# An attention block on one core: the pair sums of probabilities are dropped, and norm work moves from VectorE to ScalarE and GpSimd

## The reference, cut to what matters

```python
mod = silu(c) @ wmod                      # six rows of 512 for each batch: sa, ca, ga, sb, cb, gb
h = layernorm(x) * (1 + ca) + sa          # the "head" of a batch
q, k, v = split(h @ W_qkv + b_qkv)        # q and k are then turned (rope)
att = softmax(causal(q @ k.T / sqrt(32)))
x = x + ga * ((att @ v) @ W_proj + b_proj)
h = layernorm(x) * (1 + cb) + sb          # the "tail" of a batch
y = layernorm(h) * ln_g + ln_b            # (the reference's routed part adds nothing to h here)
out = x + gb * y
```

## Time and profile before

| | us |
|---|---|
| median of three timed runs | 3326.5 (3326.02 to 3330.23) |
| the profiled execution, its own time | 3331.65 |
| its span, first to last instruction | 3329.9 |

### The profile page before, as it was taken

The page is one execution under the profiler, slowest core; times in us unless marked ns, Lnnn a source line. Parts: engine busy times, 40 slices in busy tenths (PEclk is TensorE's granted clock), DMA queues, the critical chain, the costliest instruction groups (busy, mean ns, idle before and its releaser), DMA issues.

```text
span 3329.9 us, 59017 instructions
## 1 busy us (share of the span) xinstructions
PE 3022.2 (91%) x21664; PEld 1154.2 (35%) x21664; DVE 2585.6 (78%) x4454; ACT 1759.3 (53%) x3411; POOL 1575.2 (47%) x1489
## 2 busy tenths in 40 slices
PE   3799999999989999999998999999898999999895
PEld 1323333324343433424333242433324333242221
DVE  4697777897768788897877878798776878878477
ACT  3416565656655555655455555565544555555551
POOL 2304343471616365372644726365471655627354
PEclk8759999999999999999999999999999999999997
DMA  5402030313041220413123041311314112031122
GB/s 207 106 10 66 20 69 19 92 39 75 13 103 39 70 57 23 100 39 84 39 52 93 26 94 33 80 50 39 87 33 109 42 45 72 26 77 45 48 75 69
DMA packets 180874, 205.27 MB, mean 62 GB/s; under 512 B 21460, under 2 KB 137428, under 8 KB 179428
## 3 DMA queue, kind: packets, MB, share of 16 engines
q1 hardware_dynamic: 180584, 201.50, 23.0%
HBM read 114.09 MB, written 36.50 MB: 45 GB/s over the span
## 4 chain that ended last, share of the span: by engine, by line
PE 46%; DVE 20%; issue 16%; POOL 6%; POOLq 5%; DVEq 3%; DMA 2%; ACT 1%; SPq 1%; ACTq 0%
DVE mpart L864 11%; PE ring L1108 9%; PE ps_out L1158 9%; PE ps_scores L1144 7%; PE ps_scores L1082 6%; PE ps_den L1175 4%; PE ps_scores L1094 3%; PE ring L1130 3%; PE ps_den L1181 3%; POOL psum L504 3%; DVE dsum L880 2%; POOL psum L503 2%; DVE wk L908 1%; POOLq L484 1%; DVE wk L906 1%
## 5 line engine op out<-in xcount | busy, mean ns | idle before, releaser
L699 ACT ACTIVATE prob<-ps_scores 128x512 f32<-128x512 f32 (+3 forms) x2560 | 1261.8, 537 | 1128.8 <-PE ps_scores L1147 548.6
L864 DVE TENSOR_REDUCE mpart<-ring 128x1 f32<-128x512 f32 (+3 forms) x2560 | 1399.4, 599 | 277.2 <-PE ring L1108 143.0
L1108 PE MATMUL ring<-qk 96*128 96x512 f16 (+3 forms) x2560 | 877.6, 364 | 91.0 <-DVE mpart L864 79.1
L1144 PE MATMUL ps_scores<-qk 98*128 98x512 f16 (+3 forms) x2560 | 865.5, 352 | 35.5 <-ACT prob L699 31.5
L503 POOL TENSOR_TENSOR psum<-prob 128x512 f32<-128x512 f32 x360 | 482.4, 1340 | 427.3 <-ACT prob L699 296.3
L1158 PE MATMUL ps_out<-prob,v 128*32 128x512 f32 (+3 forms) x5120 | 608.0, 547 | 0.0
L1108 PEld LDWEIGHTS ring<-qk 96*128 96x128 f16 x2560 | 235.7, 97 | 909.8 <-DVE mpart L864 666.7
L504 POOL TENSOR_TENSOR psum<-prob 128x512 f32<-128x512 f32 x360 | 481.8, 1338 | 0.0
L1144 PEld LDWEIGHTS ps_scores<-qk 98*128 98x128 f16 x2560 | 246.5, 98 | 347.0 <-ACT prob L699 213.1
L1082 PE MATMUL ps_scores<-hT,wg 128*128 128x512 f16 x1536 | 345.2, 382 | 3.5 <-POOL hT L494 3.5
L522 POOL TENSOR_TENSOR xs<-xs,bc 128x512 f32<-128x512 f32 x60 | 77.1, 1286 | 553.7 <-DMA xs<-in_L_attn_x_dram 552.8
(11 more groups left out here) (122 smaller groups left out, 2568.2 us busy)
## 6 DMA issues: line engine op xcount, KB each, us to landing
qk<-half SPq DMA_DIRECT2D x384, 128.0 KB, 3.5
turn<-in_rope_dram SPq DMA_DIRECT2D x64, 512.0 KB, 4.6
xs<-in_L_attn_x_dram SPq DMA_DIRECT2D x124, 256.0 KB, 2.8
attn_out_T<-ot SPq DMA_DIRECT2D x63, 256.0 KB, 2.1
otin<-attn_out_T SPq DMA_DIRECT2D x30, 512.0 KB, 4.7
out_dram<-x SPq DMA_DIRECT2D x60, 256.0 KB, 2.1
wg<-w_qkv_halves SPq DMA_DIRECT2D x16, 768.0 KB, 5.6
qk<-in_L_wmod_dram SPq DMA_DIRECT2D x1, 6144.0 KB, 26.7
```

Of the source, the lines that this page charges most:

```text
L699: act.activation(prob[:, s % 3, p, h % 2, 0:w], ps_scores[(HG * s + h) % NBK][:, 0:w], ACT.Exp, scale=SCALE).then_inc(exp_done, 1)
L864: dve.tensor_reduce(mpart[:, h, qt, kc:kc + 1], ring[n % NBK][:, 0:w], AX.X, ALU.max).then_inc(ring_free, 1)
L1108: mm = pe.matmul(ring[n % NBK][:, 0:w], qk[0:R, G % 2, 0, h, qt * P:(qt + 1) * P], qk[0:R, G % 2, 1, h, kc * QC:kc * QC + w], start=True, ...
L1144: mm = pe.matmul(ps_scores[k % NBK][:, 0:w], qk[0:RM, par, 1, h, kt * P:(kt + 1) * P], qk[0:RM, par, 0, h, cq * QC + q0:(cq + 1) * QC], st ...
```

## The change

1. `add_pair`, `psum2` and the semaphores `pair_sum` and `pair_used` go. Every step has its own denominators quad from `prob`.
2. `prob` has four buffers; ScalarE waits for the denominators of the step four before.
3. Order on TensorE: values and denominators of the step before stand together, after scores 3, in every step.
4. Tail norms: VectorE keeps the gate product and both statistics. GpSimd makes at step +2 the inverse deviation and minus mean times it; ScalarE applies both in one instruction at step +3 (`tail_scaled1`), between the exponentials of heads 1 and 2; GpSimd multiplies and adds the rows at +4 (`tail_rows1`); statistics at +6; GpSimd again at +6 (`tail_shifts2`); ScalarE at +7 (`tail_scaled2`); GpSimd the last two instructions at +8 (`tail_rows2`).
5. Head in g = 2: ScalarE does the norm (after the exponential of head 2 in the odd step before the tile's) and `head_evac` (in the odd step after it, behind the exponential of head 0). The ring bank of a head tile is therefore freed by ScalarE; `bank_free` on TensorE waits for `ring_free` or `turn_free` accordingly. GpSimd's low half is one step later.
6. The loads of the tile at step 2 are issued inside the projection stretch, at chunk 2, ahead of the load of the last rope table.
7. The planner's loads follow: the added quad, and VectorE without the moved work. The batch loops are counted in one running number of ring uses.

```diff
-    PAIRS = [s for s, (cq, kt) in enumerate(STEPS) if kt < TPC * cq and kt % 2 == 0]
-    NP = len(PAIRS)
+    NPB = 4
+    FIRST_TAIL = 2
@@ product_load, vector_load
-            if STEPS[s - 1][1] >= TPC * STEPS[s - 1][0]:
-                load += 4.2 * width(s - 1)
-        return load + 4.2 * (s - 3 in PAIRS) + 6 * (s in tail) + 2 * (s in head)
+            load += 4.2 * width(s - 1)
+        return load + 6 * (s in tail) + 2 * (s in head)
-        load += sum(c * (s - at in tail) for at, c in ((0, 1.7), (2, 2.2), (4, 4), (6, 2.2), (8, 4)))
-        return load + 2.7 * (s in head) + 2.2 * (s + 2 in head) + (s + 1 in head)
+        load += sum(c * (s - at in tail) for at, c in ((0, 1.7), (2, 2.2), (6, 2.2)))
+        return load + 2.2 * (s + 2 in head)
@@ SyncE, qkv
+                    if c == 2:
+                        tail_load()
                     if G < NG * B - 1 or c < NC_ - 1:
                         load_turn(NC_ * G + c + 1)
@@ GpSimd
+            def minus_mean(to, mean, inverse):
+                pool.tensor_tensor(to, mean, neg_one[:], ALU.mult)
+                pool.drain()
+                return pool.tensor_tensor(to, to, inverse, ALU.mult)
+            def tail_shifts1(b, t):
+                i = t % 2
+                pool.wait_ge(tail_stats1, NT * b + t + 1)
+                inv_std(rstd[:, i, :], mv[:, i, :])
+                pool.drain()
+                minus_mean(shift[:, i, :], mv[:, i, 0:1], rstd[:, i, :]).then_inc(tail_rstd1, 1)
+                pool.tensor_tensor(xs[:, i, :], x1[:, i, :], bc[:, 5, :], ALU.add)
+            def tail_rows1(b, t):
+                i = t % 2
+                pool.wait_ge(tail_n1, NT * b + t + 1)
+                pool.tensor_tensor(wk[:, i, :], wk[:, i, :], bc[:, 2, :], ALU.mult)
+                pool.drain()
+                pool.tensor_tensor(wk[:, i, :], wk[:, i, :], bc[:, 3, :], ALU.add).then_inc(tail_h2, 1)
...
-                        if s - 1 in PAIRS and nxt:
-                            add_pair(G, PAIRS.index(s - 1))
-                        for stage in (0, 1, 3):
-                            if s - 2 * stage in tail:
+                        for stage in (0, 2, 4, 6, 8):
+                            if s - stage in tail:
@@ ScalarE
-                            act.wait_ge(prob_used, wait_value(S - 2 if s >= 3 else NS * G))
+                            act.wait_ge(prob_used, wait_value(S - NPB + 1))
...
+                            if h == 1 and s - 3 in tail_at(g, b == 0, last):
+                                tail_scaled1(b - 1, tail_at(g, b == 0, last)[s - 3])
+                            if h == 1 and s - 7 in tail_at(g, b == 0, last):
+                                tail_scaled2(b - 1, tail_at(g, b == 0, last)[s - 7])
+                            if h == 0 and s - 1 in head:
+                                head_evac(b + 1, head[s - 1], turns[s - 1])
+                            if h == 2 and s + 1 in head:
+                                head_normed(b + 1, head[s + 1])
+            def head_evac(b, t, use):
...
+                act.wait_ge(head_done, NT * b + t - 1)
+                act.wait_ge(ring_full, use + 1)
+                for k in range(KC):
+                    scaled = act.activation(x1[:, t % 2, k * P:(k + 1) * P], ring[use % NBK][:, k * P:(k + 1) * P],
+                                            ACT.Identity, bias=colmod[:, 0, k:k + 1], scale=colmod[:, 1, k:k + 1])
+                scaled.then_inc(turn_free, 1)
+            def tail_scaled1(b, t):
+                i = t % 2
+                act.wait_ge(tail_rstd1, NT * b + t + 1)
+                act.activation(wk[:, i, :], x1[:, i, :], ACT.Identity, bias=shift[:, i, :], scale=rstd[:, i, :]).then_inc(
+                    tail_n1, 1)
@@ TensorE
+            def bank_free(use):
+                if use >= NBK and freed_by[use - NBK] == "dve":
+                    pe.wait_ge(ring_free, freed[use - NBK])
+                elif use >= NBK:
+                    pe.wait_ge(turn_free, NT + freed[use - NBK])
...
-                            if place == (3 if s > 1 and STEPS[s - 1][1] == 0 else 2) and s > 0:
-                                values(G, par, s - 1, nxt)
                             if place == 3 and s > 0:
-                                denominators(G, s - 1, nxt)
+                                values(G, par, s - 1)
+                                denominators(G, s - 1)
```

More of the change, by code:

```diff
@@ L255, in adaln_block_kernel @@
                              "tail_stats2", "tail_rstd2", "tail_done"))
+        tail_n1, tail_h2, tail_n2 = (sem(n) for n in ("tail_n1", "tail_h2", "tail_n2"))
         def job_base(b):
             return NT // 2 if isinstance(b, int) and b == 0 else NT * b
[L262 to L270, removed]
+        freed_by = ["dve"] * (NS * HG)
+        for b in range(B):
+            for g in range(NG):
+                last = b == B - 1
+                tail, head, own = tail_at(g, b == 0, last), head_at(g, last), own_at(g, last)
+                plan = unit_plan(tail, head)
+                for s in range(NS):
+                    freed_by += ["dve"] * (0 if last and g == NG - 1 else len(plan[s]))
+                    freed_by += ["dve"] * ((s in tail) + (s in own)) + ["act"] * (s in head)
+        freed_by += ["dve"] * TPC
+        counts = {"dve": 0, "act": 0}
+        freed = []
+        for who in freed_by:
+            counts[who] += 1
+            freed.append(counts[who])
         assert NC_ == 4 and NBK == 3
@@ L277, in batches @@
         def batches(body):
-            for b in range(B - 1):
-                body(b, first=b == 0, last=False)
-            return body(B - 1, first=False, last=True)
+            n = NS * HG
+            for b in range(B):
+                n = body(b, b == 0, b == B - 1, n)
+            return n
         block = ctx.enter_context(nc.Block())
@@ L397, in end_attention, with body, tail_load @@
                     ot_ld[t // 2 % 2], 16)
-            def body(b, first, last):
+            def body(b, first, last, n):
                 for g in range(NG):
+                    tail, head, own = tail_at(g, first, last), head_at(g, last), own_at(g, last)
+                    def tail_load(at):
+                        if at in tail:
+                            t = tail[at]
+                            Z = NT * (b - 1) + t
+                            if t < 2 or (t < 2 * T0 + 2 and t >= 2 * T0 and not last):
+                                tail_loads(b - 1, t, head_norm, NT * (b + 1 + (t > 1)))
+                            else:
+                                tail_loads(b - 1, t, tail_done, Z - 1)
                     if last and g == NG - 1:
@@ L407, in body @@
                         load_group((g + 2) % NG)
-                    tail, head, own = tail_at(g, first, last), head_at(g, last), own_at(g, last)
                     for s in range(NS):
@@ L414, in body @@
                             store_ot(b, g - (cq == NC_ - 1), cq)
[L415 to L421 removed]
+                        if s + 2 != FIRST_TAIL:
+                            tail_load(s + 2)
                         if s - 9 in tail:
@@ L450, in _ @@
             load_turn(0)
[L451 removed]
+            qkv(0, None, lambda: None)
             load_group(1)
@@ L685, in body @@
                         maxima(G)
+                    tail, head, own = tail_at(g, b == 0, last), head_at(g, last), own_at(g, last)
+                    plan = unit_plan(tail, head)
+                    turns = {}
                     for s, (cq, kt) in enumerate(STEPS):
@@ L688, in body @@
                         S = NS * G + s
+                        n += (len(plan[s]) if nxt else 0) + (s in tail) + (s in own)
+                        if s in head:
+                            turns[s] = n
+                            n += 1
                         for h in range(HG):
```

264 lines of the change are left out of this document (123 added, 141 removed).

## The result

| | us | runs |
|---|---|---|
| before, same chip | 3328.36 (3326.02 to 3331.13) | 4 |
| after | 3392.47 (3391.41 to 3399.30) | 4 |
| ratio | 1.0197 [1.0179, 1.0214] | |
| forecast | 3312 (3262 to 3374) | |

The change makes the kernel 64 us slower. The forecast was 16 us faster, and the time lies outside its range.

The account below looks back on a forecast made before the run. TensorE, busy 91%, was taken as the bound, with 232.5 us of waits beyond plain groups. Waits -121, plain-group costs +102, last group +5: -14 us against the profiled 3331.65; from the median 3312 us, range 3262 to 3374.

Parts of the forecast that it names:

- The plain group: Group without tail or head: added quads and bursts raise it from 166.9 by 6.8 to 173.7 us; 15 groups +102.
- The last group: Group without units: scores 3 waits for head 0's exponential, +0.19 us in 24 steps, +5 us.
- The head: Head groups: TensorE waits 1.5 us every odd step for ScalarE's bank release; 20.8 us of waits replace 14.1; near 205 us.
- The collisions of stages: Tail groups: GpSimd's stage 0 ahead of another tile's stage 6 delays ScalarE 1.0 to 1.3 us, 24 times.
- Tail ... I let them go. What is late next: GpSimd's five stages: Tail groups: old TensorE waits dropped; late stages and the rest cost 3.1 us (g = 0 or 1) or 6.5 (six tiles), 38.1 in all.
- The rope table: Each g = 0: last table lands late behind the early loads, delaying scores 2 of step 0; 3.6 us each, 10.8 in all.
- 8.65 us pause before the first product: Each g = 0: TensorE's pause plus the slow product at lower clock, 10 us three times, inside the 232.5 us of waits.
- A: Rival, slower: ScalarE waits for norm values at all tail tiles; 36 more places give 3359 us; chance 0.30.
- B: Rival, much faster: head's bank isn't waited for, 7 us of waits per head group, 3271 us; chance 0.15.
- C: Rival, slower: nothing overlaps, 180 more quads at 1.09 us and no wait given back, 3522 us; chance 0.02.
- D: Rival, no change: early loads don't come early, SyncE held before chunk 2's end, 3331 us; chance 0.05.
- the bursts: Five units behind the quads make the next step's third unit wait about 0.2 us; +2.0 us a plain group (0 to +4).

Follow-up runs that it names:

- e10: e1's kernel (quads alone) with the first tail loads at chunk 3 and the output first on GpSimd: 3266.01 us, ratio 0.9818.
- e4: Changed kernel with the head's norm and read-out back on VectorE: 3372.61 us, ratio 1.0145.
- e6: Changed kernel with e2's and e3's edits, head still on ScalarE, units beyond the second behind the quads after a head tile: 3263.15 us, ratio 0.9813.
- e9: e6's kernel with GpSimd's tail stages ordered 6, 2, 4, 8, 0 within a step: 3240.85 us, ratio 0.9742.
- e3: Changed kernel with the output's normalisation and low half ahead of the tail's stages on GpSimd: 3324.31 us, ratio 0.9997.
- e1: Kernel before with the quads alone: no pair sums, four prob buffers, values and denominators together, planner's load following: 3357.85 us, ratio 1.0099.
- e7: Kernel before with first tail loads at chunk 3 and the output ahead of pair sums and stages on GpSimd: 3271.27 us, ratio 0.9835.
- e8: Kernel before with only the output ahead of pair sums and tail stages on GpSimd: 3319.06 us, ratio 0.9979.
- e2: Changed kernel with the first tail loads at chunk 3, behind the last rope table, instead of chunk 2: 3360.11 us, ratio 1.0104.

## Why the prediction was wrong

**The plain group: right.** 173.7 us forecast; 174.3, 174.9 and 173.3 measured, in e10 174.1, 175.1 and 173.2 with nothing else of the change.

**The last group: too dear.** I took +5 us for it. From the turning of its maxima (3123.6 us before, 3183.6 after) to the end it takes 206.3 us before and 206.0 after. The group before it, with six tiles, went from 205.2 to 207.2 us, where I had 196: it belongs to the tail groups that failed.

**The head: right, in mechanism and size.** 205 us forecast, 201.8 to 202.9 measured; 1.5 us a tile forecast for the third unit, 53.9 / 48 = 1.1 us measured, somewhat less. e4 and e6 show the cause from both sides: another reader of the bank, or a later use of it, takes the wait away. I had put the three heads at +14 us each against before, where +10.9 were measured.

**The collisions of stages: right in sum.** e9 gives 22 us for what I priced at 24 x about 1.1.

**"Tail ... I let them go. What is late next: GpSimd's five stages": the step that failed.** The prediction looked at what the *stages* deliver late, and not at what stands behind them in the same queue. `out_norm` and `out_low` were in GpSimd's body behind the stages, and its "1.3 where the output's normalisation is in GpSimd's queue too" was the wrong way round: it counted the output as delaying the norm, while the stages, one of which waits for the product at the step's end and another of which is 2 x 1.27 us, delayed the output. ScalarE's `leave` and `out_high` wait for it in the midst of the exponentials. The wait was in the trace of before, 59.6 us of ScalarE's, among those that I let go; it became 76.2 us (60.1 and 16.1), and TensorE's wait for exponentials 105.9 us where it had been 31.5. e3 shows 68 us for it, and with that one thing undone the kernel comes within 5 us of the forecasts of the tail groups: pairs 387.9, 383.9 and 383.8 (383 forecast), six tiles 195.2, 197.9 and 200.2 (196), and 3324 us in all against 3312. The condition was there to be read: I followed ScalarE's order behind the read-out and TensorE's behind a late bank, and did not follow GpSimd's behind a waiting stage. The moved stages are not all of it: the same order is worth 7 us before, about 44 with the quads alone (an estimate, from e1, e10, e7 and e8) and 68 with the norms moved too; how the quads make it dear stays open.

**The rope table: mechanism right, size off.** Forecast 3.6 us for each g = 0, bound 5; TensorE's pauses were 7.39, 5.70 and 5.04, two others of 2.97 and 3.55 us were in groups for which I had nothing, and the lower clock after each came on top: 32 us (e2) for 10.8. My 11.2 us from issue to landing were about right (10.85 to its use). But I counted them from 947.60, the table's issue time before: SyncE now issues three loads ahead of it, from 977.13 on, so its own issue is 3.6 us later, and those 3.6 us were left out.

**A price left out of every wait.** Many of the longer pauses are followed by a stretch at half clock (the counts are below). I had that for the 8.65 us pause before the first product, and for no pause of my own forecast. In the pair it is 8.1 of 19.6 us. It does not explain the whole kernel: after the first 260 us the kernel before was at half clock for 139 us and the one after for 126.

**The rivals.** A in its own form falls: 70 us of ScalarE's idleness at L808 remain in e3, at a kernel 68 us faster, and TensorE's share of them is the 22 us of e9. My mark for A ("idle before the tail norms for more than 60 us") would have proved it wrongly; an idle line of an engine that isn't the bound is no price. What happened is of A's kind, ScalarE held by GpSimd, but at another value. B falls for the kernel as changed; with the bank wanted later, in e6, its head group of 166.9 + 6.8 + 9.9 + 7 = 190.6 us is missed by 2. C falls: e10 shows that the quads cost nothing net, once the two orders are mended; with the orders as they were they cost 32 us (e1). Of the Trainium skill's rule that the engine with the highest occupancy is relieved first (Perfetto Trace Analysis, "Identifying the Most-Contended Engine") the prediction asked whether it speaks against the change: it doesn't here, as TensorE was given 180 quads and e10 is 5 us below e7; the engine to look at was GpSimd, at 27%. D falls: the loads came early enough, and the first product had no pause. The range's lower end was mis-added: B's 3271 us with no wait from the bursts (15 x 2.0) is 3241, not 3262; the measured time lies beyond the other end.

What stays open: e6's head groups are 3 to 7 us above what I expected. That e1 gives back 6 us in the six-tile groups by VectorE's room and not by the pair sums' absence on GpSimd was not told apart.

## What to carry to other kernels

When work is given to an engine that executes in order, list what was already in its queue *behind* the place, and who waits for that; the new work's own deadline is the smaller question. A short instruction that someone waits for goes ahead of a long one that no one waits for, and one that itself must wait goes last: these two sentences were worth 90 us of 3392 here (e3 and e9), and the change itself, with them, the loads one chunk later and the head tile's bank wanted later, came to 2.6% below the kernel before (e9). Of that 1.6% is what the two orders give to the kernel before by themselves (e7), and 0.9% what e9 has over e7: a change is to be held against the old kernel with the same repairs. Adding work to the busiest engine is free in those stages in which it waits for a slower partner (e10), so price it by stage.

## What the hardware showed that was not expected

- A quad that takes 1.04 us took 1.91 after a pause of 2.05 us, and 1.94 instead of 1.07 after one of 7.39. It is no fixed rule: in the kernel after, past the first 232 us, the granted clock fell in or within 1.4 us after all six pauses of 3 us or more, but only nine of the sixteen from 2 to 3 us (one more lay within a stretch that was slow already). A pause of 2.29 us at 1273.9 had it, one of 2.30 us at 2083.8 had not. The time at half clock after the first 260 us was 139 us before, 126 in the kernel after, 89 in e3 and 48 in e6.
- 512 KB issued behind 1536, 512 and 256 KB (`bc`, `otin`, `xs`) on the same queue were in use 10.85 us after their issue, where the median landing of that load over the kernel is 4.7 us.
- Two full f32 quads in a row, 0.88 us from start to start where one alone takes 1.00, hold that in an ordinary group too (1340.62 and 1341.50 above).
